# Expert blocks with the weights as the loaded operand of gate and up

## Chip, cores and metric

The kernel runs on one core of one Trainium2 chip. The time is device time of one execution in microseconds; the three runs before the change took 1558.29, 1562.61 and 1563.08 us, so the median is 1562.61.

## What is computed

Four sub-layers follow each other on 2048 tokens of 512 numbers, each added to its input and normalised: a linear attention, a feed-forward layer with int8 weights, a cumulative gate, and a mixture of 32 experts. The change touches the last one:

```python
router_probs = jax.nn.softmax(x @ gate_weight.T)
# 8 experts a token, some rerouted by a similarity matrix; combine = weight of each expert for each token
def expert_step(y, params):
    wgu, wd, cw = params          # (384, 512), (512, 192), (2048,)
    gu = x @ wgu.T
    g, u = jnp.split(gu, 2, axis=-1)
    h = jax.nn.silu(g) * u
    y = y + h @ wd.T * cw[:, None]
```

## The kernel before, in words

The program is written engine by engine; each engine runs its instructions in the order of the code, and semaphores join them. The first three sub-layers and the routing take the first 930 us or so. Routing sorts the 2048 x 8 pairs of token and expert into 159 blocks (NBLK) of 128 rows with one expert each. `every_block` (line 348 is its loop) then runs the same code for each block on every engine: eight blocks written out, a loop of eight blocks a turn, and the rest written out.

Numbers are held as two halves of 16 bits, high and low, so a product is three matmuls: high x high, high x low, low x high. `products` lists them with the four pieces of 128 of the 512 inputs: 12 for gate and up.

For a block k, POOL gathers its 128 rows (L1794). TensorE turns them (`gather_transposes`, L880, eight turns: four pieces, high and low), VectorE copies them out (L1341). `gate_up` (L889) is on TensorE the product with the tokens as loaded operand and the 384 columns of gate and up streaming past; tokens come out on partitions. ScalarE makes silu of the gate columns (L1619), VectorE multiplies by up and by the token's weight for this expert (L1351), ScalarE copies the high half (helper line L1380), VectorE subtracts for the low half (L1353, L1354). `h_transposes` (L899) turns h, three turns, ScalarE copies that out (L1380, the 384-wide form), and `expert_down` (L910) makes five matmuls of 512 columns. ScalarE copies y out with a constant scale (L1380, 512 wide), POOL adds its rows into memory (L1801).

On TensorE the code of one block k is in this order: down of block k-3; the waits for the expert's weights (L923, L924) and the turned rows; two thirds of gate/up; the turns of block k+1's rows; the last third; the turns of h of block k-1. The wait in `h_transposes` is for `h_lo`, VectorE's last subtraction.

The weights of the experts lie in eight slots. Which slot a block uses is known only when the kernel runs: the expert's number comes out of packed words, which TensorE and VectorE read into registers (L357, `load_words`; TensorE at the first and third block of eight), and the place of a piece is the slot's number times its size plus a constant:

```python
def weights(sl, j, c0, n):
    return Wslot[:, bass.ds(sl * (2 * WCOLS) + (j * WCOLS + c0), n)]
```

Such a place is computed by an instruction of the engine's sequencer, called ISA in the order of instructions and FUSED_REGOPS in the trace, ahead of the first matmul that reads it.

Of the kernel before, what the change touches and what calls it, by code (L numbers as in the profile page):

```python
# [24 lines left out]
P = 128  # L25
# [59 lines left out]
def build(nc, ins, out):  # L85
    ctx = ExitStack()
    with ctx:
# [88 lines left out]
        def wc(a, k, c0, n):  # L176
# [61 lines left out]
        xTb = [r.take([2 * KD, P], F16) for _ in range(2)]  # L238
        sgD = [r.take([DFF], F32) for _ in range(2)]
        h32 = [r.take([DFF], F32) for _ in range(2)]  # L240
        hB = [r.take([3 * P], F16) for _ in range(2)]
        hT = [r.take([3, P], F16) for _ in range(2)]
# [44 lines left out]
        w_in, xg_in, y_out = sem("w_in"), [sem(f"xg_in{i}") for i in range(NG)], [sem(f"y_out{i}") for i in range(2)]  # L287
        xt_ready, xt_sb, gu_ready, sg_ready, h_ready, h_hi, h_lo, ht_ready, ht_sb, blk_done, y_sb = (sem(n) for n in (
            "xt_ready", "xt_sb", "gu_ready", "sg_ready", "h_ready", "h_hi", "h_lo", "ht_ready", "ht_sb", "blk_done", "y_sb"))
        fin_in, fin_first, sum_ready = [sem(f"fin_in{i}") for i in range(4)], sem("fin_first"), sem("sum_ready")  # L290
# [301 lines left out]
        def _(pe):  # L592
# [292 lines left out]

            def gate_up(k, sl, some):
                d = bank[2 + k.u % 2][:, 0:2 * DFF]
                for a, b, kd in some:
                    mm = pe.matmul(d, xTb[k.u % 2][:, a * KD + kd, :], weights(sl, b, kd * 2 * DFF, 2 * DFF),  # L889
                                   start=(a, b, kd) == (0, 0, 0), stop=(a, b, kd) == (1, 0, KD - 1))  # L890
                return mm

            def h_transposes(k):
                pe.wait_ge(h_lo, k.i + 1)
                if not k.before(2):
                    pe.wait_ge(ht_sb, k.i - 1)
                d = bank[4 + k.u % 2][:, :].bitcast(F16)
                for c in range(3):
                    mm = pe.transpose(d[:, c * P:(c + 1) * P], hB[k.u % 2][:, c * P:(c + 1) * P], ident16[:, :])  # L899
                mm.then_inc(ht_ready, 1)  # L900

            def expert_down(k, sl):
                pe.wait_ge(ht_sb, k.i + 1)
                if not k.before(2):
                    pe.wait_ge(y_sb, k.i - 1)
                d = bank[6 + k.u % 2][:, :]
                base = KD * 2 * DFF
                order = ((1, 0, base), (1, 1, base), (0, 0, base), (2, 0, base + DIM), (2, 1, base + DIM))
                for n, (c, j, c0) in enumerate(order):
                    mm = pe.matmul(d, hT[k.u % 2][:, c, :], weights(sl, j, c0, DIM), start=n == 0, stop=n == 4)  # L910
                mm.then_inc(blk_done, 1)
# [4 lines left out]
            def expert_block(k, fresh, last=False):  # L916
                if fresh:
                    held["packs"] = load_words(pe.engine, k, 0, 1)
                e = expert_of(held["packs"], k.u)
                if not k.before(3):  # L920
                    expert_down(k.at(-3), expert_of(held["packs"], k.u - 3) % NSLOT)
                sl = e % NSLOT
                pe.wait_ge(w_in, e * 32 + 32)  # L923
                pe.wait_ge(xt_sb, k.i + 1)  # L924
                if not k.before(2):
                    pe.wait_ge(h_ready, k.i - 1)
                gate_up(k, sl, products[:6])
                if k.u == 2:
                    held["packs"] = held["packs"] + load_words(pe.engine, k, 1, 2)
                gate_up(k, sl, products[6:8])  # L930
                if not last:
                    gather_transposes(k.at(1))
                gate_up(k, sl, products[8:]).then_inc(gu_ready, 1)
                if not k.before(1):
                    h_transposes(k.at(-1))

# [3 lines left out]
            every_block(pe, 8, expert_block, 8)  # L940
            final = [Blk(0, NBLK - j, 8) for j in (3, 2, 1)]
            expert_down(final[0], expert_of(held["packs"], NBLK % 8 - 3) % NSLOT)
            h_transposes(final[2])
            expert_down(final[1], expert_of(held["packs"], NBLK % 8 - 2) % NSLOT)
            expert_down(final[2], expert_of(held["packs"], NBLK % 8 - 1) % NSLOT)


        @block.vector
        def _(dve):
# [334 lines left out]
            choices(3)  # L1284
            own.did(dve.memset(xgs[:, :, DIM:XROW], 0.0))
            one_hots(2, 0, 12)
            candidates(3)
# [55 lines left out]
            def expert_block(k, fresh, last=False):  # L1343
                if not last:
                    xt_evac(k.at(1))
                if fresh:
                    mine["packs"] = load_words(dve.engine, k, 0, 2)
                cw = xg[k.u % NG].bitcast(F32)[:, DIM:XROW][:, bass.ds(expert_of(mine["packs"], k.u), 1)]
                h, split = h32[k.u % 2], hB[k.u % 2]
                dve.wait_ge(sg_ready, k.i + 1)  # L1350
                dve.scalar_tensor_tensor(h, bank[2 + k.u % 2][:, DFF:2 * DFF], cw, sgD[k.u % 2], ALU.mult, ALU.mult).then_inc(h_ready, 1)  # L1351
                dve.wait_ge(h_hi, k.i + 1)
                dve.tensor_tensor(split[:, 0:P], h[:, 0:P], split[:, P:2 * P], ALU.subtract)  # L1353
                dve.tensor_tensor(split[:, 2 * P + 64:3 * P], h[:, P:DFF], split[:, 2 * P:2 * P + 64], ALU.subtract).then_inc(h_lo, 1)  # L1354

# [17 lines left out]
        def _(act):  # L1373
# [228 lines left out]

            def ht_evac(k):
                act.wait_ge(ht_ready, k.i + 1)
                if not k.before(2):
                    act.wait_ge(blk_done, k.i)
                copy(hT[k.u % 2].rearrange("p c n -> p (c n)"), bank[4 + k.u % 2][:, :].bitcast(F16)[:, 0:3 * P]).then_inc(ht_sb, 1)
# [22 lines left out]
            ht_evac(Blk(0, NBLK - 1, 8))  # L1630
            y_evac(Blk(0, NBLK - 2, 8))
# [276 lines left out]
```

## Time and profile before

| | |
|---|---|
| median of three runs | 1562.61 us |
| profiled execution | 1556.97 us, its span 1555.1 us |
| TensorE busy | 1405.1 us, 90% of the span |
| VectorE, ScalarE, GpSimd busy | 909.7, 662.7, 763.6 us |
| mean granted TensorE clock | 0.954 |

PE is TensorE's matmuls, PEld its weight loads, which run beside them; PEldq and PEq are its sequencer, which issues both, computes addresses and waits for semaphores, and whose rows count in no busy time. DVE is VectorE, ACT ScalarE, POOL GpSimd. A matmul's row lasts from its issue to its modelled end, so rows overlap: its own cost in a run of them is the step from start to start. The clock is a share of the upper level.

### The profile page before, as it was taken

The numbers are of one execution on the slowest core, as the hardware profiler recorded it, in microseconds if no ns is written. First come the engines' busy times: TensorE is split into PE (matmuls) and PEld (weight loads), VectorE is DVE, ScalarE is ACT, GpSimd is POOL, SyncE is SP. The second block draws the span as 40 slices with busy tenths as digits, with TensorE's granted clock in tenths as the row PEclk, the third lists the DMA queues.
The fourth block names the chain that finished last, engine by engine and source line by source line (L and its number), as shares of the span: only waits on it lengthen the run. The fifth ranks groups of instructions, "written<-read, shape, count | busy, mean of one in ns | idle before, by whom it ended". The sixth has DMA issues, their size and how long they took to land.

```text
span 1555.1 us, 31694 instructions
## 1 busy us (share of the span) xinstructions
PE 1405.1 (90%) x10327; PEld 771.1 (50%) x10328; DVE 909.7 (58%) x1826; ACT 662.7 (43%) x1250; POOL 763.6 (49%) x691
## 2 busy tenths in 40 slices
PE   5799899799999999999886359999999999999990
PEld 2455555444444444445443226666666666666650
DVE  7677566676757676635988864444444444444435
ACT  6332222455454545423444424444444444444443
POOL 3565454510100101233645446777777677777655
PEclk9999999899999999999998569999999999999995
DMA  8777666689696969432303636888888988776767
GB/s 273 170 156 187 120 111 122 150 297 311 223 295 224 299 229 297 169 107 82 83 18 100 200 120 121 174 172 199 192 192 175 207 188 191 142 113 90 177 80 230
DMA packets 213452, 271.72 MB, mean 175 GB/s; under 512 B 133993, under 2 KB 135561, under 8 KB 212368
## 3 DMA queue, kind: packets, MB, share of 16 engines
q1 hardware_dynamic: 177776, 211.40, 46.6%
q0 software_dynamic: 35616, 59.58, 23.5%
q8 instruction: 31, 0.51, 0.1%
q14 instruction: 29, 0.24, 0.0%
HBM read 158.92 MB, written 101.71 MB: 168 GB/s over the span
## 4 chain that ended last, share of the span: by engine, by line
PE 73%; DVE 13%; DMA 5%; issue 2%; ACT 2%; POOL 2%; SPq 2%; DVEq 0%; ACTq 0%; POOLq 0%
PE bank L889 20%; PE bank L910 11%; PE bank L716 7%; PE bank L722 6%; PE bank L739 6%; PE bank L598 6%; PE bank L880 5%; PE bank L606 4%; DMA ARENA<-ARENA 4%; PE bank L673 2%; PE bank L899 2%; DVE ARENA L1251 1%; PE bank L818 1%; DVE bs L956 1%; DVE WA L1197 1%
## 5 line engine op out<-in xcount | busy, mean ns | idle before, releaser
L889 PE MATMUL bank<-ARENA,XT 128*128 x1908 | 364.0, 327 | 2.5 <-issue 1.4
L1801 POOL DMA_INDIRECT accs<-X,WA x159 | 252.3, 1587 | 89.6 <-issue 42.0
L889 PEld LDWEIGHTS bank<-ARENA,XT 128*128 128x128 f16 x1908 | 180.4, 98 | 124.5 <-issue 8.5
L1341 DVE COPY XT<-bank 128x1024 f16<-128x1024 f16 x159 | 110.0, 692 | 179.0 <-PE bank L880 146.2
L1794 POOL DMA_INDIRECT XT<-x_rows,WA x159 | 166.6, 1048 | 97.1 <-issue 42.1
L910 PE MATMUL bank<-ARENA,XT 128*128 x795 | 197.4, 379 | 0.8 <-issue 0.7
L1380 ACT ACTIVATE ARENA<-ARENA 128x512 f16<-128x512 f32 (+2 forms) x128 | 89.2, 708 | 231.7 <-DVE ARENA L1099 130.6
L1619 ACT ACTIVATE XT<-bank 128x192 f32<-128x192 f32 x159 | 52.5, 330 | 286.7 <-PE bank L889 232.7
L598 PE MATMUL bank<-XT,STG 128*128 128x512 f16 x640 | 152.4, 386 | 7.7 <-DVE ARENA L1145 7.6
L1647 POOL TENSOR_TENSOR rstd<-mv,mhalf 128x1 f32<-128x1 f32 x28 | 5.7, 202 | 281.9 <-DVE mv L959 281.9
L606 PE MATMUL bank<-WA,XT 128*128 128x512 f16 x540 | 126.2, 384 | 0.0
L716 PE MATMUL bank<-XT,WA 128*128 (+1 forms) x512 | 122.3, 382 | 3.4 <-issue 3.4
L739 PE MATMUL bank<-ARENA 128*128 128x512 f16 x512 | 121.1, 379 | 3.5 <-DVE ARENA L1105 3.4
L1351 DVE SCALAR_TENSOR_TENSOR XT<-bank,XT 128x192 f32<-128x192 f32 x159 | 66.4, 418 | 98.2 <-ACT XT L1619 65.4
L722 PE MATMUL bank<-XT,ARENA 128*128 (+1 forms) x512 | 120.9, 379 | 0.0
L598 PEld LDWEIGHTS bank<-XT,STG 128*128 128x128 f16 x640 | 62.8, 99 | 81.2 <-DVE ARENA L1145 9.0
L880 PE MATMUL bank<-ident,XT 128*128 128x128 f16 x1272 | 97.8, 220 | 5.6 <-DMA XT<-x_rows,WA 5.6
L1656 POOL TENSOR_TENSOR ARENA<-X,ARENA 128x512 f16<-128x512 f32 (+1 forms) x48 | 63.6, 1338 | 78.4 <-ACT ARENA L1380 78.4
L910 PEld LDWEIGHTS bank<-ARENA,XT 128*128 128x128 f16 x795 | 71.6, 98 | 57.7 <-issue 1.8
L880 PEld LDWEIGHTS bank<-ident,XT 128*128 128x128 f16 x1272 | 85.0, 98 | 25.7 <-issue 6.2
L1380 ACT ACTIVATE X<-bank 128x512 f32<-128x512 f32 x159 | 93.3, 587 | 2.8 <-PE bank L910 1.3
L953 DVE SCALAR_TENSOR_TENSOR WA<-ARENA,WA 128x1280 f16<-128x1280 f32 x48 | 73.3, 1527 | 25.5 <-ACT WA L1380 25.5
(244 smaller groups left out, 2184.6 us busy)
## 6 DMA issues: line engine op xcount, KB each, us to landing
w_scratch<-WA SPq DMA_DIRECT2D x64, 640.0 KB, 3.9
ARENA<-w_scratch SPq DMA_DIRECT2D x64, 640.0 KB
ARENA<-w_exp SPq DMA_DIRECT2D x48, 640.0 KB, 5.3
WA<-w_exp SPq DMA_DIRECT2D x16, 640.0 KB, 5.0
ARENA<-ARENA SPq DMA_DIRECT2D x32, 256.0 KB, 3.5
accs<-ARENA SPq DMA_DIRECT2D x20, 256.0 KB, 3.4
X<-x SPq DMA_DIRECT2D x4, 1024.0 KB, 6.8
ARENA<-wc SPq DMA_DIRECT2D x8, 512.0 KB, 6.0
```

Source lines behind the costliest of these rows:

```text
L598: mm = pe.matmul(dst, wa(a, k), wb(b, k), start=n == 0, stop=n == 3 * KD - 1)
L606: mm = pe.matmul(bank[j][:, :], XT[:, a, k, tk], Wqkv[:, b, k, j * DIM:(j + 1) * DIM], start=n == 0, stop=n == 3 * KD - 1)
L716: mm = pe.matmul(bank[0][:, :], Wg[:, n % KD, m * P:(m + 1) * P], XT[:, n // KD, n % KD, tk], start=n == 0, stop=n == 2 * KD - 1)
L722: mm = pe.matmul(bank[1 + m % 2][:, :], Wu[:, n % KD, m * P:(m + 1) * P], XT[:, n // KD, n % KD, tk], start=n == 0, stop=n == 2 * KD - 1)
L739: mm = pe.matmul(bank[4 + tt][:, :], fB[:, m % 2, a, tt * P:(tt + 1) * P], Wd[:, m, :], start=m == 0 and a == 0, stop=m == NM - 1 and a == 1)
L880: mm = pe.transpose(d[:, c * P:(c + 1) * P], xg[k.u % NG].bitcast(F16)[:, c * P:(c + 1) * P], ident16[:, :])
L889: mm = pe.matmul(d, xTb[k.u % 2][:, a * KD + kd, :], weights(sl, b, kd * 2 * DFF, 2 * DFF), start=(a, b, kd) == (0, 0, 0), stop=(a, b, kd) ...
L910: mm = pe.matmul(d, hT[k.u % 2][:, c, :], weights(sl, j, c0, DIM), start=n == 0, stop=n == 4)
L1341: dve.tensor_copy(xTb[k.u % 2].rearrange("p c n -> p (c n)"), bank[k.u % 2][:, :].bitcast(F16)).then_inc(xt_sb, 1)
L1380: return act.activation(dst, src, ACT.Copy, scale=scale)
L1794: pool.indirect_dma_start(xg[i % NG], None, xrows, bass.IndirectOffsetOnAxis(blkidx[:, i:i + 1], 0), bounds_check=TOK - 1, oob_is_err=Fals ...
L1801: pool.indirect_dma_start(accs, bass.IndirectOffsetOnAxis(blkout[:, i:i + 1], 0), yD[i % 8], None, compute_op=ALU.add).then_inc(y_out[i % ...
```

## The change

Gate and up are computed with the weights as the loaded operand and the tokens streaming, so features come out on partitions, in three parts of 128 (gate 0 to 127; gate 128 to 191 with up 0 to 63; up 64 to 191). h then lies as the down product needs it: its turns and their copy go. The multiply by up is three instructions, two of them between different halves of the partitions. The token's weight, which can't be multiplied along partitions now, goes into the scale of the copy of y. The down product runs two blocks behind in place of three.

```diff
-        sgD = [r.take([DFF], F32) for _ in range(2)]
-        h32 = [r.take([DFF], F32) for _ in range(2)]
-        hB = [r.take([3 * P], F16) for _ in range(2)]
+        sgD = [r.take([2 * P], F32) for _ in range(2)]
+        h32 = [r.take([2 * P], F32) for _ in range(2)]
+        cwS = small[:, 108:116]
...
-            def gate_up(k, sl, some):
-                d = bank[2 + k.u % 2][:, 0:2 * DFF]
+            def gate_up(k, sl, part, some):
+                d = bank[2 + k.u % 2][:, part * P:(part + 1) * P]
                 for a, b, kd in some:
-                    mm = pe.matmul(d, xTb[k.u % 2][:, a * KD + kd, :], weights(sl, b, kd * 2 * DFF, 2 * DFF),
+                    w = weights(sl, b, kd * 2 * DFF + part * P, P)
+                    mm = pe.matmul(d, w, xTb[k.u % 2][:, a * KD + kd, :],
                                    start=(a, b, kd) == (0, 0, 0), stop=(a, b, kd) == (1, 0, KD - 1))
...
-            def h_transposes(k):
...
             def expert_down(k, sl):
-                pe.wait_ge(ht_sb, k.i + 1)
+                pe.wait_ge(h_lo, k.i + 1)
...
-                if not k.before(3):
-                    expert_down(k.at(-3), expert_of(held["packs"], k.u - 3) % NSLOT)
+                if not k.before(2):
+                    expert_down(k.at(-2), expert_of(held["packs"], k.u - 2) % NSLOT)
...
-                gate_up(k, sl, products[:6])
+                gate_up(k, sl, 0, products)
                 if k.u == 2:
                     held["packs"] = held["packs"] + load_words(pe.engine, k, 1, 2)
-                gate_up(k, sl, products[6:8])
+                gate_up(k, sl, 1, products)
                 if not last:
                     gather_transposes(k.at(1))
-                gate_up(k, sl, products[8:]).then_inc(gu_ready, 1)
-                if not k.before(1):
-                    h_transposes(k.at(-1))
+                gate_up(k, sl, 2, products).then_inc(gu_ready, 1)
...
+            for h in h32:
+                own.did(dve.memset(h[:, P:2 * P], 0.0))
...
+                dve.tensor_scalar(cwS[:, k.u % 8:k.u % 8 + 1], cw, 1 / (WS * WS), None, ALU.mult)
                 dve.wait_ge(sg_ready, k.i + 1)
-                dve.scalar_tensor_tensor(h, bank[2 + k.u % 2][:, DFF:2 * DFF], cw, sgD[k.u % 2], ALU.mult, ALU.mult).then_inc(h_ready, 1)
+                dve.tensor_tensor(h[0:64, 0:P], d[64:128, P:2 * P], sg[0:64, 0:P], ALU.mult)
+                dve.tensor_tensor(h[64:128, 0:P], d[0:64, 2 * P:3 * P], sg[64:128, 0:P], ALU.mult)
+                dve.tensor_tensor(h[0:64, P:2 * P], d[64:128, 2 * P:3 * P], sg[0:64, P:2 * P], ALU.mult).then_inc(h_ready, 1)
                 dve.wait_ge(h_hi, k.i + 1)
-                dve.tensor_tensor(split[:, 0:P], h[:, 0:P], split[:, P:2 * P], ALU.subtract)
-                dve.tensor_tensor(split[:, 2 * P + 64:3 * P], h[:, P:DFF], split[:, 2 * P:2 * P + 64], ALU.subtract).then_inc(h_lo, 1)
+                dve.tensor_tensor(turned[:, 0, :], h[:, 0:P], turned[:, 1, :], ALU.subtract)
+                dve.tensor_tensor(turned[64:128, 2, :], h[0:64, P:2 * P], turned[0:64, 2, :], ALU.subtract).then_inc(h_lo, 1)
...
-                copy(yD[k.u % 8], bank[6 + k.u % 2][:, :], 1 / (WS * WS)).then_inc(y_sb, 1)
+                act.activation(yD[k.u % 8], bank[6 + k.u % 2][:, :], ACT.Copy, scale=cwS[:, k.u % 8:k.u % 8 + 1]).then_inc(y_sb, 1)
...
-                act.activation(sgD[k.u % 2], bank[2 + k.u % 2][:, 0:DFF], ACT.Silu, scale=1 / WS).then_inc(sg_ready, 1)
-                if not k.before(1):
-                    ht_evac(k.at(-1))
+                act.activation(sgD[k.u % 2], bank[2 + k.u % 2][:, 0:2 * P], ACT.Silu, scale=1 / WS).then_inc(sg_ready, 1)
                 act.wait_ge(h_ready, k.i + 1)
                 if not k.before(2):
-                    act.wait_ge(ht_ready, k.i - 1)
-                copy(hB[k.u % 2][:, P:2 * P + 64], h32[k.u % 2]).then_inc(h_hi, 1)
+                    act.wait_ge(blk_done, k.i)
+                copy(hT[k.u % 2][:, 1:3, :].rearrange("p c n -> p (c n)"), h32[k.u % 2]).then_inc(h_hi, 1)
```

TensorE's instructions from the eighth gate/up matmul of a block of the loop to the next block's down product, before; `ident` is the unit matrix for a turn, `bank` the result, XT the tokens, ARENA the weight slots, and in brackets stands what is waited for:

```order
L889 ISA
L889 MATMUL bank<-ARENA,XT 128x384
L875 ISA
L880 MATMUL bank<-ident,XT 128x128 [waits xt_sb,xg_in1]
L880 MATMUL bank<-ident,XT 128x128 x7
L889 MATMUL bank<-ARENA,XT 128x384 x4
L899 MATMUL bank<-ident,XT 128x128 [waits ht_sb,h_lo]
L899 MATMUL bank<-ident,XT 128x128 x2
L905 REGISTER_ALU [waits ht_sb]
L910 ISA [waits y_sb]
L910 REGISTER_ALU
```

The same stretch of the same block with the change, from the end of the second part of gate/up (it begins and ends between addresses that go on in the same way):

```order
L890 ISA
L890 MATMUL bank<-XT,ARENA 128x128 x5
L875 ISA
L880 MATMUL bank<-ident,XT 128x128 [waits xt_sb,xg_in1]
L880 MATMUL bank<-ident,XT 128x128 x7
L890 ISA
L890 MATMUL bank<-XT,ARENA 128x128
L890 ISA
L890 MATMUL bank<-XT,ARENA 128x128
```

Behind the turns, where four matmuls without an ISA stood, the third part begins with its own eight, one ahead of each of its first eight matmuls; the last of these is the `x5` row, the eighth and the four that use places again. The turns of h are gone, and `h_lo` is waited for at the down product:

```order
L890 ISA
L890 MATMUL bank<-XT,ARENA 128x128 x5
L897 REGISTER_ALU [waits h_lo]
L902 ISA [waits y_sb]
L902 REGISTER_ALU
L902 MATMUL bank<-ARENA,XT 128x512
```

In the eight blocks of the loop's body there are 64 rows `L889 ISA` before and 192 rows `L890 ISA` with the change; the 32 of the down product stay.

On VectorE one block of the loop is before:

```order
L1341 COPY XT<-bank 128x1024 [waits gu_ready,xt_ready]
L1351 ISA [waits sg_ready]
L1351 SCALAR_TENSOR_TENSOR XT<-bank,XT 128x192
L1353 TENSOR_TENSOR XT<-XT 128x128 [waits h_hi]
L1354 TENSOR_TENSOR XT<-XT 128x64
```

and with the change:

```order
L1330 COPY XT<-bank 128x1024 [waits gu_ready,xt_ready]
L1339 ISA
L1339 TENSOR_SCALAR small<-XT 128x1
L1341 TENSOR_TENSOR XT<-bank,XT 64x128 [waits sg_ready]
L1342 TENSOR_TENSOR XT<-bank,XT 64x128
L1343 TENSOR_TENSOR XT<-bank,XT 64x128
L1345 TENSOR_TENSOR XT<-XT 128x128 [waits h_hi]
L1346 TENSOR_TENSOR XT<-XT 64x128
```

The address of the token's weight is now computed before the wait for `sg_ready`, and three multiplies stand behind that wait in place of one.

## Rows read from the trace of the kernel before

**Rows 1.** The page: busy time by engine; the chain that ended last, by engine.

```profile
PE 1405.1 (90%) x10327; PEld 771.1 (50%) x10328; DVE 909.7 (58%) x1826; ACT 662.7 (43%) x1250; POOL 763.6 (49%) x691
...
PE bank L889 20%; PE bank L910 11%; PE bank L716 7%; PE bank L722 6%; PE bank L739 6%; PE bank L598 6%; PE bank L880 5%; PE bank L606 4%; DMA ARENA<-ARENA 4%; PE bank L673 2%; PE bank L899 2%; DVE ARENA L1251 1%; PE bank L818 1%; DVE bs L956 1%; DVE WA L1197 1%
```

**Rows 2.** Stretches: us, busy PE, PEld, DVE, ACT, POOL, clock, DMA share, GB/s.

```profile
0.00:100.00 100.00, 73.09 (x762) 38.23 (x767) 73.45 (x100) 48.14 (x64) 49.08 (x38) 0.93 0.79 205
...
985.00:1483.00 498.00, 496.73 (x3808) 310.18 (x3806) 209.16 (x544) 218.29 (x544) 358.12 (x272) 1.00 0.82 168
```

**Rows 3.** The chain in order of time, one block: start, us, what.

```profile
1204.11 1.30 PE bank L889 x8
1205.41 0.45 PE bank L880 x8
1205.86 0.65 PE bank L889 x4
1206.51 0.17 PE bank L899 x3
1206.67 1.08 PE bank L910 x5
```

**Rows 4.** Lines L889 (whole span), L923 (984 to 1483): durations min/median/max, first, last start.

```profile
L889 PE MATMUL bank<-ARENA,XT x1908: 326/326/524, 928.1 to 1509.6; 128*128 x191
L889 PEldq FUSED_REGOPS  x1272: 46/46/96, 928.0 to 1507.9; - x182
...
L923 PEldq FUSED_REGOPS  x136: 83/135/142, 987.0 to 1479.8; - x136
```

**Rows 5.** The same view: runs of addresses ahead of the array, L889 and L606.

```profile
L889 PEldq FUSED_REGOPS  x8: 46/46/91, 1213.9 to 1214.9; - x8
...
L889 PEldq FUSED_REGOPS  x6: 46/46/57, 1217.9 to 1218.5; - x6
...
L606 PEldq FUSED_REGOPS  x8: 46/46/51, 72.5 to 73.4; - x8
```

**Rows 6.** The same view: sequencer rows around 951, 1220 and 1230 us.

```profile
L877 PEldq EVENT_SEMAPHORE  x1: 51/51/51, 951.0 to 951.0; - x1
...
L896 PEldq EVENT_SEMAPHORE  x1: 51/51/51, 951.2 to 951.2; - x1
...
L348 PEldq ALU_OP  x1: 32/32/32, 1219.4 to 1219.4; - x1
...
L903 PEldq FUSED_REGOPS  x1: 47/47/47, 1220.5 to 1220.5; - x1
...
L923 PEldq FUSED_REGOPS  x2: 83/90/98, 1228.4 to 1231.5; - x2
...
L357 PEldq FUSED_REGOPS  x2: 46/98/151, 1229.5 to 1230.0; - x2
...
L357 PEldq SEQ_ASSERT  x1: 18/18/18, 1230.2 to 1230.2; - x1
```

**Rows 7.** The same view: L637 and L638 at 78 to 80 us; groups by line: one load.

```profile
L637 PE MATMUL bank<-ARENA x16: 219/219/219, 78.4 to 80.1; 128*128 128x128 f16 x16
...
L638 PE MATMUL bank<-ARENA x16: 219/219/219, 78.5 to 80.1; 128*128 128x128 f16 x16
...
L880 PEld LDWEIGHTS bank<-ident,XT 128*128 128x128 f16 x1054 | 69.9, 98 | 16.4
```

**Rows 8.** Groups of VectorE and ScalarE, 1000 to 1480 us: busy, mean ns, idle before.

```profile
L1341 DVE COPY XT<-bank 128x1024 f16<-128x1024 f16 x131 | 90.6, 692 | 140.7 <-PE bank L880 115.2 <-issue 25.4
L1351 DVE SCALAR_TENSOR_TENSOR XT<-bank,XT 128x192 f32<-128x192 f32 x131 | 54.8, 418 | 80.6 <-ACT XT L1619 52.5 <-issue 28.1
L1353 DVE TENSOR_TENSOR XT<-XT 128x128 f16<-128x128 f32 x131 | 38.3, 293 | 56.9 <-ACT XT L1380 50.5 <-issue 6.4
...
L1380 ACT ACTIVATE X<-bank 128x512 f32<-128x512 f32 x131 | 76.9, 587 | 1.1 <-PE bank L910 0.4
L1380 ACT ACTIVATE XT<-bank 128x384 f16<-128x384 f16 x131 | 63.7, 486 | 5.5 <-PE bank L899 4.9
```

More of the change, by code:

```diff
@@ L287, in build @@
         w_in, xg_in, y_out = sem("w_in"), [sem(f"xg_in{i}") for i in range(NG)], [sem(f"y_out{i}") for i in range(2)]
-        xt_ready, xt_sb, gu_ready, sg_ready, h_ready, h_hi, h_lo, ht_ready, ht_sb, blk_done, y_sb = (sem(n) for n in (
-            "xt_ready", "xt_sb", "gu_ready", "sg_ready", "h_ready", "h_hi", "h_lo", "ht_ready", "ht_sb", "blk_done", "y_sb"))
+        xt_ready, xt_sb, gu_ready, sg_ready, h_ready, h_hi, h_lo, blk_done, y_sb = (sem(n) for n in (
+            "xt_ready", "xt_sb", "gu_ready", "sg_ready", "h_ready", "h_hi", "h_lo", "blk_done", "y_sb"))
         fin_in, fin_first, sum_ready = [sem(f"fin_in{i}") for i in range(4)], sem("fin_first"), sem("sum_ready")
@@ L884, in weights, with expert_down @@
                 return Wslot[:, bass.ds(sl * (2 * WCOLS) + (j * WCOLS + c0), n)]
-            def gate_up(k, sl, some):
-                d = bank[2 + k.u % 2][:, 0:2 * DFF]
+            def gate_up(k, sl, part, some):
+                d = bank[2 + k.u % 2][:, part * P:(part + 1) * P]
                 for a, b, kd in some:
-                    mm = pe.matmul(d, xTb[k.u % 2][:, a * KD + kd, :], weights(sl, b, kd * 2 * DFF, 2 * DFF),
+                    w = weights(sl, b, kd * 2 * DFF + part * P, P)
+                    mm = pe.matmul(d, w, xTb[k.u % 2][:, a * KD + kd, :],
                                    start=(a, b, kd) == (0, 0, 0), stop=(a, b, kd) == (1, 0, KD - 1))
                 return mm
-            def h_transposes(k):
+            def expert_down(k, sl):
                 pe.wait_ge(h_lo, k.i + 1)
[L895 to L902, printed above, removed]
-                pe.wait_ge(ht_sb, k.i + 1)
                 if not k.before(2):
@@ L940, in _ @@
             every_block(pe, 8, expert_block, 8)
[L941 to L945, printed above, removed]
+            for j in (2, 1):
+                expert_down(Blk(0, NBLK - j, 8), expert_of(held["packs"], NBLK % 8 - j) % NSLOT)
         @block.vector
@@ L1348, in expert_block @@
                 cw = xg[k.u % NG].bitcast(F32)[:, DIM:XROW][:, bass.ds(expert_of(mine["packs"], k.u), 1)]
-                h, split = h32[k.u % 2], hB[k.u % 2]
+                d, sg, h, turned = bank[2 + k.u % 2], sgD[k.u % 2], h32[k.u % 2], hT[k.u % 2]
+                dve.tensor_scalar(cwS[:, k.u % 8:k.u % 8 + 1], cw, 1 / (WS * WS), None, ALU.mult)
                 dve.wait_ge(sg_ready, k.i + 1)
-                dve.scalar_tensor_tensor(h, bank[2 + k.u % 2][:, DFF:2 * DFF], cw, sgD[k.u % 2], ALU.mult, ALU.mult).then_inc(h_ready, 1)
+                dve.tensor_tensor(h[0:64, 0:P], d[64:128, P:2 * P], sg[0:64, 0:P], ALU.mult)
+                dve.tensor_tensor(h[64:128, 0:P], d[0:64, 2 * P:3 * P], sg[64:128, 0:P], ALU.mult)
+                dve.tensor_tensor(h[0:64, P:2 * P], d[64:128, 2 * P:3 * P], sg[0:64, P:2 * P], ALU.mult).then_inc(h_ready, 1)
                 dve.wait_ge(h_hi, k.i + 1)
-                dve.tensor_tensor(split[:, 0:P], h[:, 0:P], split[:, P:2 * P], ALU.subtract)
-                dve.tensor_tensor(split[:, 2 * P + 64:3 * P], h[:, P:DFF], split[:, 2 * P:2 * P + 64], ALU.subtract).then_inc(h_lo, 1)
+                dve.tensor_tensor(turned[:, 0, :], h[:, 0:P], turned[:, 1, :], ALU.subtract)
+                dve.tensor_tensor(turned[64:128, 2, :], h[0:64, P:2 * P], turned[0:64, 2, :], ALU.subtract).then_inc(h_lo, 1)
             xt_evac(Blk(0, 0, 8))
@@ L1601, in _ @@
             copy(region, bank[2][:, 256:256 + NBLK]).then_inc(region_sb, 1)
[L1603 to L1607, printed above, removed]
             def y_evac(k):
@@ L1629, in _ @@
             every_block(act, 8, expert_block)
-            ht_evac(Blk(0, NBLK - 1, 8))
             y_evac(Blk(0, NBLK - 2, 8))
```

## The prediction

> **What bounds the kernel now.** I read the page first: TensorE is busy 90% of the span, and the chain that ended last goes through it most, with the expert blocks' gate/up line L889 at its head [rows 1]. The change touches only these blocks, so next I read the table of stretches: from 985 to 1483 us TensorE has work 496.7 of 498.0 us at granted clock 1.00, its upper level of 2.4 GHz [rows 2]. Then the chain in order of time shows one block with no gap in it: 8 gate/up matmuls of 384 columns in 1.30 us, 8 turns of gathered rows in 0.45, 4 more gate/up in 0.65, 3 turns of h in 0.17, 5 down matmuls in 1.08, together 3.65 us [rows 3]. That is also the pace of the address row L923, issued once a block: 135 steps from 987.0 to 1479.8, 3.65 us each [rows 4]. So the array's columns set the block today: 162 ns a gate/up matmul, 56 ns a turn, 216 ns a down matmul [rows 3].
>
> What a busy array hides is who feeds it. TensorE's sequencer issues in order, and a block's weights lie in a slot that a register names, so an address is computed (FUSED_REGOPS in the trace, ISA in the order of instructions) before a matmul that reads a new place of the slot: 1272 for L889, 8 a block [rows 4]. Each lasts 46 ns, but they don't follow each other every 46 ns. Where the sequencer runs free, ahead of the array, eight in a row start from 1213.9 to 1214.9 and six from 1217.9 to 1218.5; in the attention stage, where the loaded operand is the one with the register, eight go from 72.5 to 73.4 [rows 5]. That is 0.14, 0.12 and 0.13 us a step; I take 0.125, since the 0.14 includes a longer first row. The same pace holds with one matmul behind each address or several (in the 72.5 run, five follow the fourth), so the address has the price, not the matmul: from L877 to L896 twelve load-and-matmul pairs without a new address are issued in 0.2 us [rows 6], of which 0.05 is the wait's own row: 0.012 us a pair.
>
> Today this is hidden. In a block where the sequencer was catching up, L923 follows L923 after 3.1 us, of which 0.75 goes to a word load (1229.5 to just past 1230.2) [rows 6]: 2.35 us of issue against 3.65 of columns.
>
> **The change part by part.**
>
> *Gate/up turned round.* 12 matmuls of 384 columns become 36 of 128. Columns: 36 x 0.056 = 2.02 us against 12 x 0.1625 = 1.95, +0.07 [rows 3]. That each carries its own weight load costs nothing on the array: in the attention stage 32 such pairs, L637 and L638 in turn, start from 78.4 to 80.1, some 55 ns each, with loads of 98 ns beside them [rows 7]. Against that stands a rule of the Trainium skill, TensorE: Matmul & The Clock Gate, section Back-to-back issue gap: a sustained stream of load-and-matmul pairs at 128 columns runs at about 81 ns a pair, which as an estimate would make this block 44 x 0.081 + 1.08 = 4.64 us on the array and the kernel about 1715 us. The 32 pairs disagree, and I go by them.
>
> Issue: 24 new addresses a block in place of 8 (each third of the 384 features has eight places, and the low-part product reuses the last four). 16 x 0.125 = +2.0 us. Eight more pairs without an address add 8 x 0.012 = 0.1.
>
> *h_transposes and their copy go.* TensorE loses 3 x 0.056 = 0.17 us of columns, its sequencer about 0.1 us (three pairs and a wait, by the L877 row). ScalarE loses a copy of 0.49 us [rows 8]; the array never stood still for it, so that is worth nothing.
>
> *Sum for a block.* Array: 2.02 + 0.45 + 1.08 = 3.55 us. Issue: 2.35 + 2.0 + 0.1 - 0.1 = 4.35. The sequencer becomes the bound. It then also shows what it hid so far, once in eight blocks: the loop's branch and first word load, 1219.4 to 1220.5 or 1.1 us, and the second load, 0.75 [rows 6]; 1.85 / 8 = 0.23. Together 4.58 us; the branch's first row partly overlaps what the block before had queued, so I take 4.56.
>
> *VectorE.* One multiply of 0.42 us becomes three of half the partitions, by the rows between 0.29 and 0.42 each, and a one-column scaling; one subtraction grows from 64 to 128 columns. Sums 0.7 to 1.1 us more a block, on an engine with 209 of 498 us busy [rows 2, 8]: hidden while its chain stays short. *ScalarE*: a sigmoid-times-x pass 64 columns wider, a copy 64 wider, the token weight as scale of the copy that it did anyway: under 0.2 us, and 0.49 gone. Two fills before the blocks are under 0.5 us. POOL's and SP's instructions stay.
>
> *The down product moves* from three blocks behind to two, and its wait for h_lo now stands on the sequencer before everything of the block. Behind it queue the five down matmuls, then gate/up. After the last gate/up of block k-2 comes the whole issue of block k-1, 4.56 us, before that wait. The chain meanwhile is activation 0.49 at most, three multiplies 1.26, copy 0.49, two subtractions 0.58: 2.8 us, and 4.1 if both engines first finish another copy (0.59 and 0.69) [rows 8]. It fits; cost nothing, and up to 0.5 us in the one block of eight with VectorE's own word load if it doesn't (10 us in all).
>
> **Total.** 159 blocks x (4.56 - 3.65) = +145 us on the profiled execution's 1557.0: 1702 us. The median of the three runs is 5.6 above that execution and all lie within 1558 to 1563, so I say **1704 us**. An address at 0.12 or 0.13 moves this by 24 x 0.005 x 159 = 19 us either way, the rounding of the other rows by 16: 1670 to 1738.
>
> **The rivals.**
>
> *The array keeps the pace (the other side).* If an address cost the sequencer little more than its 46 ns, the array would bound: 3.55 us, 159 x 0.10 = 16 us less, 1541. It decides at (3.55 - 2.56) / 16 = 62 ns an address, 2.56 being all that is issued without the 16. For it: the 46 ns of the rows, and that the trace may itself slow this sequencer. Against it: three runs of addresses in two stages, none under 0.12 [rows 5]. Between 62 and 69 ns it would be no change.
>
> *TensorE's clock falls.* The array would have 3.55 of 4.56 us to do, 78%. From 0 to 100 us, with 73% busy, the granted clock was 0.93 [rows 2], so some 0.14 of the time at the lower level of 1.2 GHz. There a block's columns take 7.1 us, more than its issue: 5% on 725 us, 38 us more, 1740. Against it: no idle stretch is longer than an address's step.
>
> *Weight loads don't overlap.* At 98 ns a pair [rows 7] the array takes 44 x 0.098 + 1.08 = 5.39 us a block, +277 us, 1834. The 32 pairs at 56 speak against it. The rule named above lies between the two.
>
> *The chain is late after all*: 1704 plus up to 10, as above.
>
> **How the numbers follow.** Forecast 0.78; clock 0.07; loads 0.03; chain 0.03; array bound 0.06, and 0.03 for an address price in between, near no change. A measurement tells about 0.3% from no change here. Faster 0.06, same 0.02, slower 0.92 (the in-between case split between the last two). The range, 1660 to 1745, holds the forecast with its roundings, the chain and the clock case; it leaves out the array bound, the loads and some of the edges, under 0.2.
>
> **What would show it.** L890 addresses at 24 a block, 3816 in all, 0.12 to 0.13 us apart throughout, not only in short runs; the gate/up matmuls with addresses starting 0.125 us apart and the four without 0.056; one block 4.3 to 4.4 us, a pair of blocks of eight a full us longer; TensorE idle with "issue" as its reason; the turns of h gone from every list; VectorE some 0.7 to 1.1 us busier a block and waited for by nobody. Wrong would be: gate/up pairs 56 ns apart with the block at 3.55 us; addresses closer than 0.1 us; h_lo or xt_sb named as what TensorE waited for; a granted clock under 0.95 through the blocks.

## The result: slower, 1723.4 us

The changed kernel takes 1723.36 us (median of four runs, 1722.40 to 1724.31) against 1562.84 us before in the same measurement: a ratio of 1.1033, with a 95% interval of 1.1019 to 1.1048. The forecast was 1704, between 1660 and 1745. The page of the profile after, busy time by engine and the head of the chain by line:

```profile
PE 1530.2 (89%) x13666; PEld 953.0 (55%) x13667; DVE 1022.9 (59%) x2305; ACT 626.8 (36%) x1091; POOL 763.8 (44%) x691
...
PE bank L890 26%; PE bank L902 10%; PE bank L716 5%; PE bank L722 5%; PE bank L739 5%; PE bank L598 5%; PE bank L880 4%; PE bank L606 4%; DMA ARENA<-ARENA 2%; PE bank L673 2%; DVE ARENA L1238 1%; ACT ARENA L1372 1%; DVE bs L943 1%; PE bank L818 1%; DVE WA L1184 1%
```

By the share of busy time nothing has happened: TensorE 89% where it was 90% [rows 1]. A matmul's row lasts 219 ns however soon the next one follows, so rows that start 125 ns apart still touch. The table of stretches has the same trap (columns as in [rows 2]):

```profile
985.00:1483.00 498.00, 474.19 (x5238) 364.99 (x5235) 239.28 (x748) 146.49 (x321) 282.20 (x214) 1.00 0.70 143
```

474 of 498 us have a matmul under way, but only 107 blocks go through the stretch in place of 136. The granted clock is 1.00 in both. What changed is seen in the rows of the gate/up line and of the address row that is issued once a block (durations min/median/max, first and last start; then what TensorE's idle time waited for):

```profile
L890 PE MATMUL bank<-XT,ARENA x5724: 219/219/314, 933.3 to 1676.3; 128*128 128x128 f16 x198
L890 PEldq FUSED_REGOPS  x3816: 46/46/96, 933.1 to 1676.0; - x191
its engine sat idle before it (us, times) until:
  issue: 44.3, 140
  DVE XT L1330: 4.3, 4
...
L915 PEldq FUSED_REGOPS  x159: 82/135/162, 932.1 to 1672.5; - x159
```

There are 3816 addresses, 24 a block, each 46 ns long as before [rows 4]. The blocks' own row goes 158 steps in 740.4 us, so a block takes **4.69 us** over all and 4.66 in the loop, in place of 3.65 [rows 4]. Idle time of TensorE is "issue", hardly ever another engine. The chain in order of time shows where a block's time lies:

```profile
1256.60 1.08 PE bank L902 x5
1257.68 2.07 PE bank L890 x24
1259.74 0.45 PE bank L880 x8
1260.19 0.71 PE bank L890 x12
1260.90 1.08 PE bank L902 x5
1261.98 2.04 PE bank L890 x24
1264.02 0.45 PE bank L880 x8
1264.46 0.71 PE bank L890 x12
1265.17 0.03 issue
1265.20 1.25 PE bank L902 x5
1266.45 2.07 PE bank L890 x24
1268.52 0.45 PE bank L880 x8
1268.96 0.80 PE bank L890 x12
1269.76 1.28 issue
1271.04 1.24 PE bank L902 x5
```

The first two thirds of gate/up, 24 matmuls with 16 addresses, take 2.04 to 2.07 us where their columns need 24 x 0.056 = 1.34: this is the pace of addresses. The turns, which need one address at most, stay at 0.45 and let the sequencer get a little ahead; the last third uses that up and takes 0.71. From one down product to the next it is 4.30 us in the first two blocks, and 5.84 in the one that holds the loop's branch and first word load.

### The profile page after: what moved, and what is told of

It is laid out like the page before. It is cut to its first block, busy times and chain, and to the rows that moved or that the text cites. A ratio compares the mean times of both kernels' runs of the same rounds, so it can differ in the third digit from the quotient of the medians.

```text
span 1722.0 us, 40922 instructions
## 1 busy us (share of the span) xinstructions
PE 1530.2 (89%) x13666; PEld 953.0 (55%) x13667; DVE 1022.9 (59%) x2305; ACT 626.8 (36%) x1091; POOL 763.8 (44%) x691
## 4 chain that ended last, share of the span: by engine, by line
PE 72%; DVE 13%; issue 5%; DMA 4%; ACT 3%; POOL 2%; SPq 1%; another core or an unknown queue 0%; DVEq 0%; ACTq 0%; POOLq 0%
PE bank L890 26%; PE bank L902 10%; PE bank L716 5%; PE bank L722 5%; PE bank L739 5%; PE bank L598 5%; PE bank L880 4%; PE bank L606 4%; DMA ARENA<-ARENA 2%; PE bank L673 2%; DVE ARENA L1238 1%; ACT ARENA L1372 1%; DVE bs L943 1%; PE bank L818 1%; DVE WA L1184 1%
## 5 line engine op out<-in xcount | busy, mean ns | idle before, releaser
L890 PE MATMUL bank<-XT,ARENA 128*128 128x128 f16 x5724 | 504.6, 223 | 13.0 <-issue 8.4
L890 PEld LDWEIGHTS bank<-XT,ARENA 128*128 x5724 | 406.9, 97 | 116.6 <-issue 35.9
L902 PE MATMUL bank<-ARENA,XT 128*128 x795 | 197.8, 379 | 27.3 <-issue 24.4
L1605 ACT ACTIVATE XT<-bank 128x256 f32<-128x256 f32 x159 | 61.1, 384 | 364.7 <-PE bank L890 243.2
L1330 DVE COPY XT<-bank 128x1024 f16<-128x1024 f16 x159 | 110.0, 692 | 134.7 <-PE bank L880 119.5
L1341 DVE TENSOR_TENSOR XT<-bank,XT 64x128 f32<-64x128 f32 x159 | 46.6, 293 | 161.9 <-ACT XT L1605 154.7
L1372 ACT ACTIVATE XT<-XT 128x256 f16<-128x256 f32 x159 | 66.2, 417 | 177.1 <-DVE XT L1343 174.1
L606 PE MATMUL bank<-WA,XT 128*128 128x512 f16 x540 | 125.3, 382 | 0.0
L902 PEld LDWEIGHTS bank<-ARENA,XT 128*128 128x128 f16 x795 | 76.8, 97 | 86.1 <-issue 36.0
L1599 ACT ACTIVATE X<-bank,small 128x512 f32<-128x512 f32 x159 | 106.5, 671 | 1.0 <-PE bank L902 1.0
L1345 DVE TENSOR_TENSOR XT<-XT 128x128 f16<-128x128 f32 x159 | 46.6, 293 | 76.7 <-ACT XT L1372 67.0
```

What stands on the lines that cost most here:

```text
L606: mm = pe.matmul(bank[j][:, :], XT[:, a, k, tk], Wqkv[:, b, k, j * DIM:(j + 1) * DIM], start=n == 0, stop=n == 3 * KD - 1)
L890: mm = pe.matmul(d, w, xTb[k.u % 2][:, a * KD + kd, :], start=(a, b, kd) == (0, 0, 0), stop=(a, b, kd) == (1, 0, KD - 1))
L1330: dve.tensor_copy(xTb[k.u % 2].rearrange("p c n -> p (c n)"), bank[k.u % 2][:, :].bitcast(F16)).then_inc(xt_sb, 1)
L1372: return act.activation(dst, src, ACT.Copy, scale=scale)
```

## The experiments

The times of all fourteen kernels, with the ratio where there is more than one run. A block is a turn of the loop divided by eight, from the trace (of e3 and e4, whole blocks from first to last address row).

| kernel | us | ratio to before (95%) | block, us |
|---|---|---|---|
| before | 1562.8 | | 3.65 |
| after | 1723.4 | 1.1033 (1.1019 to 1.1048) | 4.66 |
| e1 after, addresses packed | 1629.6 | 1.0443 (1.0421 to 1.0465) | 4.10 |
| e2 after, no gate/up addresses | 1608.8 | one run | 3.95 |
| e3 before, gate/up in thirds | 1777.6 | one run | 5.01 |
| e4 before, addresses packed | 1559.6 | 0.9986 (0.9975 to 0.9998) | 3.66 |
| e5 e1, down three behind | 1583.1 | 1.0130 (1.0108 to 1.0151) | 3.77 |
| e6 after, down three behind | 1737.2 | 1.1116 (1.1091 to 1.1141) | 4.75 |
| e7 e1, waits for its own gate/up | 1782.1 | 1.1384 (1.1355 to 1.1413) | 5.09 |
| e8 e1, three operations an address | 1722.3 | one run | 4.69 |
| e9 e1, no scatter | 1560.2 | 0.9992 (0.9980 to 1.0005) | 3.70 |
| e10 e5, reordered | 1568.9 | 1.0042 (1.0024 to 1.0061) | 3.70 |
| e11 e8, down three behind | 1692.2 | one run | 4.47 |
| e12 e10, down at the block's end | 1570.3 | 1.0064 (1.0046 to 1.0083) | 3.75 |

### e1 and e2: the addresses taken away

An address here is three operations on registers (add, times two bytes, add the base). On a view in bytes it needs one, and when all are computed together, up to six operations share an instruction: e1's trace has 5 address instructions a block for gate/up in place of 24.

```diff
 def weights(sl, j, c0, n):
-    return Wslot[:, bass.ds(sl * (2 * WCOLS) + (j * WCOLS + c0), n)]
+    return Wslot.bitcast(I8)[:, bass.ds(sl * (4 * WCOLS) + 2 * (j * WCOLS + c0), 2 * n)].bitcast(F16)
...
 pe.wait_ge(w_in, e * 32 + 32)
+for part in range(3):
+    for b in range(2):
+        for kd in range(KD):
+            pe.lower_ap(weights(sl, b, kd * 2 * DFF + part * P, P), for_matmul_weights=True)
```

> The changed kernel, with a block's 24 gate/up addresses computed together at the head of the block and the slot taken on a view in bytes, so that an address is one operation on registers in place of three: 5 address instructions a block in place of 24, the same matmuls, loads and waits. Theory A (the sequencer's addresses bound the changed block): 19 fewer addresses at 0.125 us take 2.4 us of issue from a block of 4.66 us, which leaves some 2.3, less than the array's 3.55; the array bounds again, 1723 - 159 x (4.66 - 3.55) = 1547 us, between 1540 and 1565, and gate/up matmuls start 55 to 57 ns apart. Rival B (an operand named by a register, or a new weight load for each 128 columns, is what takes the array 0.125 us): nothing changes, 1715 to 1730. Rival C (the down product, now two blocks behind, waits for h_lo as soon as the block is shorter): h_lo stands behind a chain of 2.4 to 2.8 us against 3.55 less what lies between; the block stops between 3.6 and 4.2 us, 1555 to 1650, and h_lo is named as TensorE's wait.

e2 takes every load from the unit matrix:

```diff
-w = weights(sl, b, kd * 2 * DFF + part * P, P)
+w = ident16[:, :]
```

> The changed kernel, with every gate/up load taken from one fixed place (the unit matrix) in place of the expert's slot: no gate/up address at all, the same number of loads, matmuls and waits. It leaves out reading the experts' gate and up weights, so gate and up are not the experts'. Theory A (addresses bound): issue about 1.6 us a block, the array bounds at 3.55 us, about 1547 us (1540 to 1565); with e1 the same within 10 us. Rival B1 (44 load-and-matmul pairs in a row cost about 0.08 us each on the array, whatever the address): block 4.6 us, about 1715. Rival B2 (it is the register in the load itself that is slow, not the instruction that computes it): e2 falls to 1547 while e1 stays near 1723.

Measured: 1629.6 and 1608.8 us. Neither stayed near 1723, so rival B falls in all its forms: the same matmuls with the same loads from the same registers go faster when fewer instructions compute addresses. The array's own pace shows in e2's chain:

```profile
1210.63 1.08 PE bank L902 x5
1211.71 1.34 PE bank L890 x24
1213.05 0.45 PE bank L880 x8
1213.50 0.67 PE bank L890 x12
```

24 load-and-matmul pairs in 1.34 us are 56 ns each, 32 with the turns behind them in 1.79. The Trainium skill, TensorE: Matmul & The Clock Gate, section Back-to-back issue gap, has about 81 ns for such a stream; this trace differs, and the measurement decides.

But neither came to 1547. In e1 the down product's idle time (view of line L902) is

```profile
L902 PEldq ALU_OP  x598: 32/32/36, 938.6 to 1581.7; - x200
L902 PEldq FUSED_REGOPS  x38: 182/188/200, 963.7 to 1557.2; - x38
its engine sat idle before it (us, times) until:
  issue: 64.0, 79
  DVE XT L1350: 42.5, 64
```

L1350 is `h_lo`, the last subtraction. Rival C is there as soon as the block gets short: the gaps ahead of the down product come to 0.40 us a block (985 to 1483 us), the loop's branch included, and to 0.08 in e9, where that wait is gone. It is a cost that the addresses had covered.

### e3 and e4: the same in the kernel before

e3 leaves the tokens as loaded operand and only cuts gate/up into thirds, so that 24 addresses are computed:

```diff
-mm = pe.matmul(d, xTb[k.u % 2][:, a * KD + kd, :], weights(sl, b, kd * 2 * DFF, 2 * DFF),
+mm = pe.matmul(d, xTb[k.u % 2][:, a * KD + kd, :], weights(sl, b, kd * 2 * DFF + part * P, P),
```

> The kernel before, with tokens still as loaded operand, the turns of h kept and the down product three blocks behind, but gate/up in three parts of 128 columns, one after the other: 36 matmuls and 24 addresses a block in place of 12 and 8, nothing else changed. Theory A (addresses bound): the block is as slow as the changed kernel's plus the issue of the turns of h, 4.66 to 4.8 us, so 1563 + 159 x (1.01 to 1.15) = 1724 to 1746. Rival (the weights as loaded operand, or the new chain behind them, made the changed kernel slow): columns 36 x 0.056 against 12 x 0.1625 are 0.07 us a block more, so 1574 us, 1563 to 1585.

e4 packs the 8 addresses of the kernel before, with e1's view in bytes and

```diff
+for b in range(2):
+    for kd in range(KD):
+        pe.lower_ap(weights(sl, b, kd * 2 * DFF, 2 * DFF))
```

> The kernel before, with its 8 gate/up addresses a block computed together and on the byte view: 2 address instructions a block in place of 8, some 0.7 us a block less to issue, nothing else changed. If the array's columns bound it, as the prediction read it, no change: 1563 within 5 us. If issue bounds it in part (at the block in eight with the loop's branch and its first word load), up to 0.7 us in one or two of eight blocks: 14 to 28 us faster.

e3 took 1777.6 us: the loss is there without the turned product, without the new chain and with the turns of h kept, so it belongs to the 24 addresses. It went past its range, with 5.01 us a block and not 4.66 to 4.8. Two things in its sequencer's rows were not in my sum: the turns of h bring waits with them, and from a wait to the next row the sequencer needs 0.125 us, as for an address; and the step behind the last wait ahead of gate/up takes 0.34 us in the mean, where after has 0.12. e4 took 1559.6, within its 5 us: with 162 ns a matmul the addresses of before were hidden.

### e5 and e6: the down product three blocks behind again

Four buffers of h in place of two, and

```diff
-if not k.before(2):
-    expert_down(k.at(-2), expert_of(held["packs"], k.u - 2) % NSLOT)
+if not k.before(3):
+    expert_down(k.at(-3), expert_of(held["packs"], k.u - 3) % NSLOT)
```

in the packed kernel (e5) and in the changed one (e6).

> The packed kernel (e1, 1630 us, block 4.10), with the down product three blocks behind gate/up again in place of two, and four buffers of h in place of two, so that the wait for h_lo has a whole block more. In e1 some 0.5 us a block are a wait for h_lo at the head of the down product. If that wait is all that is left over the array's 3.55 us: 1547 us, 1540 to 1565. If VectorE's order (the copy of the turned rows stands behind the subtractions of the block before) then becomes what the array waits for: 3.7 to 3.9 us, 1570 to 1605, with xt_sb named. If the late product wasn't the cause: 1630.

> The changed kernel with its 24 addresses a block, the down product three blocks behind again and four buffers of h; nothing packed. Theory A (addresses bound the changed block, the wait for h_lo adds at most 0.08 us a block): 1710 to 1723. Rival (the change's loss lies in the late chain, and e1 gained only because packing moved the issue): 1560 to 1640.

With e1 and after these make a square: packing is worth 94 us two blocks behind (1723 to 1630) and 154 three behind (1737 to 1583); the third block is worth 47 us with packed addresses and costs 14 without. So the addresses bound the changed kernel, and the wait for h only decides once they are gone. e6's rival, that the late chain was the loss, is out. That e6 is slower by 14 us I had not expected. Between 985 and 1483 us the step at the wait for `h_lo` did shrink, from 0.19 to 0.13 us in the mean (10 us over 159 blocks), but the step behind the waits ahead of gate/up grew from 0.12 to 0.24 (19 us). That leaves some 5 us open. The idle time of L890 names the copied rows (L1330, `xt_sb`) 17 times, where after has 4:

```profile
  issue: 63.0, 149
  DVE XT L1330: 10.0, 17
```

e5 kept 0.22 us a block over the array's 3.55: 0.11 behind the down product (three in a turn of the loop), 0.09 ahead of it (one in each turn).

### e8 and e11: is the price by operation or by instruction?

e8 is e1 without the byte view, so 13 address instructions a block, of up to six operations; e11 is e8 with e5's edit, the down product three behind.

```diff
-return Wslot.bitcast(I8)[:, bass.ds(sl * (4 * WCOLS) + 2 * (j * WCOLS + c0), 2 * n)].bitcast(F16)
+return Wslot[:, bass.ds(sl * (2 * WCOLS) + (j * WCOLS + c0), n)]
```

> The packed kernel e1 without the view in bytes: the gate/up addresses are computed together at the head of the block, but each takes three operations on registers again, two addresses an instruction: 13 address instructions a block, all of six operations or three, in place of 24 (1723 us) or 5 (e1, 1630 us). If the price is by instruction, 0.13 us: 11 fewer than the changed kernel's, 1.4 us less issue, 3.2 us, under what bounds e1: 1630, within 15. If the price is by operation (72 and more in any case): near 1723. In between, at 0.16 us for one of six operations: 3.6 us, still under e1's 4.10.

> e8 (addresses computed together, three operations each, 13 instructions a block, 1722 us) with the down product three blocks behind. e8's 13 address instructions follow each other in 0.133 us, so the price is by instruction; but they stood as 1.7 us in one piece behind the wait for h_lo, with 1.08 us of down columns to cover them. If that place was the cause: with h_lo no longer waited for, the sequencer issues ahead and the block comes to 3.75 to 4.0 us, 1580 to 1620. If the operations cost and not the instructions: 1700 to 1725.

Both missed: 1722.3 and 1692.2 us. The price itself is in the sequencer's rows. In e8

```profile
L919 PEldq FUSED_REGOPS  x2052: 42/74/115, 930.6 to 1672.0; - x187
```

they last 74 ns in place of 46, and follow each other every 133 ns in the median (139 in e1), against 124 ns for three operations in after and 113 ns for the single ALU_OP of e1's down product. Six operations cost little more than one: the price is by instruction. The miss is in the place. Thirteen in one piece are 1.7 us, and the array had less than that in store. In e11, around 1208 us:

```profile
L902 PE MATMUL bank<-ARENA,XT x5: 379/379/379, 1207.9 to 1208.8; 128*128 x5
...
L919 PEldq FUSED_REGOPS  x13: 42/74/110, 1207.8 to 1209.5; - x13
...
L890 PE MATMUL bank<-XT,ARENA x3: 217/218/218, 1209.7 to 1209.8; 128*128 128x128 f16 x3
```

The last down matmul is over at 1209.0, the addresses at 1209.6, and the array waits 0.66 us; over the loop it is 0.78 us a block. How far the sequencer gets ahead can be counted: matmuls that stand ahead of its row in the program and start after it. At e11's wait ahead of the down product it is 17 in every block of the loop but the first of each turn, behind the branch, where it is 0. Between 985 and 1483 us it is 17 at the same place in 95 of 132 blocks of e5, and at L896 in 100 of 136 of the kernel before, never more. Seventeen matmuls of 384 columns are 2.8 us; of 128 columns, 0.95 us. In after it is 4 in 70 of 107 blocks, which are the four without an address at the end of gate/up, and 0 to 2 in the others: no lead at all. That is how an issue-bound stretch looks. (The Trainium skill, Advanced Engine Details and Errata, section Engine Queue Depths, gives TensorE a queue depth of 64; 17 matmuls with their loads are 34 instructions, so the measurement is what I go by.)

### e7 and e9: why h is late

In e1 the wait for h falls on every second block, and its cause is not the length of the chain. Around 1206 us in e1:

```profile
L890 PE MATMUL bank<-XT,ARENA x12: 219/219/219, 1205.7 to 1206.3; 128*128 128x128 f16 x12
...
L902 PE MATMUL bank<-ARENA,XT x5: 379/379/379, 1206.3 to 1207.2; 128*128 x5
...
L1609 ACT ACTIVATE XT<-bank x1: 385/385/385, 1208.0 to 1208.0; 128x256 f32<-128x256 f32 x1
...
L1788 POOL DMA_INDIRECT accs<-X,WA x1: 1589/1589/1589, 1206.5 to 1206.5; - x1
```

Gate/up is through at 1206.5, ScalarE is free, and silu (L1609) starts at 1208.0: the trace's record of semaphores has gate/up's increment, by which TensorE tells ScalarE that the product is there, at 1207.95, 1.67 us after the last matmul's start, where the prompt value is 0.23. The down product's increment, of a matmul 0.92 us later, comes 0.07 us behind it, so the array itself was not late. My first idea was that an increment waits as long as further matmuls follow; e7 lets none follow:

```diff
 if not k.before(2):
+    pe.wait_ge(gu_ready, k.i)
     expert_down(k.at(-2), expert_of(held["packs"], k.u - 2) % NSLOT)
```

> The packed kernel e1, with one wait more on TensorE's sequencer: ahead of the down product it waits for its own last gate/up matmul. In e1 the increment that tells ScalarE of that matmul comes 0.23 us after its start where the array then pauses, but 1.6 to 1.8 us after it where the next matmuls follow at once, and silu starts that much later. Theory L (an increment is told late as long as matmuls without a pause follow it; the lateness, not the chain's own 2.4 to 2.8 us, makes h_lo late): every increment comes after 0.23 us, the pause costs 0.2 to 0.35 us a block, h_lo is in time: block 3.75 to 3.9, 1580 to 1605 us, faster than e1 by an added wait. Rival (the chain is too long by itself): the pause comes on top or changes nothing, 1630 to 1660.

1782.1 us, outside the rival's range too: theory L is wrong. The increment comes late with the array at rest as well, 1.17 us after the start in the median, and now TensorE waits for it and has an empty queue behind it. Idle time ahead of the down product (L902) in e7:

```profile
its engine sat idle before it (us, times) until:
  issue: 184.8, 160
  PE bank L890: 157.3, 150
```

The other thing that runs in those spans is GpSimd's scatter of y (1.59 us) or gather (1.05 us). Between 1000 and 1450 us, of TensorE's increments that fall due (their row ends) 0.4 to 1.4 us after a scatter's start, 53 of 63 in e1 and 77 of 79 in e7 come more than 0.15 us late, mostly about 1.5 us after the scatter's start; of ScalarE's 0 of 23 and of VectorE's 0 of 59 in e1. e9 leaves the scatter out:

```diff
-pool.indirect_dma_start(accs, bass.IndirectOffsetOnAxis(blkout[:, i:i + 1], 0), yD[i % 8], None,
-                        compute_op=ALU.add).then_inc(y_out[i % 2], 16)
+pool.memset(blkout[:, i:i + 1], 0).then_inc(y_out[i % 2], 16)
```

> The packed kernel e1 (1630 us, down product two blocks behind), with GpSimd's scatter of y left out: in its place GpSimd writes zero to one column that nothing reads any more and gives the same increment. It leaves out adding the experts' results into memory, so the output has no expert part. In e1 and e7 TensorE's increments that fall due while GpSimd works on the scatter (1.59 us a block) come some 1.5 us after that scatter's start, be the array pausing or not; ScalarE's and VectorE's come at once. Theory G (the scatter holds TensorE's increments, and that makes h_lo late in e1): the gate/up increments come 0.23 us after the matmul's start, the wait for h_lo shrinks, block 3.6 to 3.8 us: 1550 to 1582. Rival (coincidence: both follow y's copy, and the increments are late for another reason): 1615 to 1640, increments still 1.5 to 1.8 us late in every second block.

1560.2 us, inside theory G's range and 69 under e1. The wait for `h_lo` is gone, once in place of 64 times (L902 again):

```profile
  issue: 22.8, 39
  DVE XT L1350: 1.5, 1
```

Gate/up's increments still come at 0.50 us in the median, not at 0.23; the gather is still there. That TensorE's late increments, and with them the wait for `h_lo`, go when the scatter goes is shown; whether GpSimd's work on it holds them or the transfers that it starts is not, since both went. Nor does the scatter do it alone. By the same count 38 of 134 are late in the kernel before and 28 of 125 in e4, where gate/up streams 384 columns, but 66 of 66 in after and 183 of 184 in e3, which keeps the tokens as loaded operand and only cuts gate/up into matmuls of 128 columns. What it is in the short matmuls that makes the difference, no run here separates.

### e10 and e12: can the turned product win?

On e5, e10 puts the next block's turns to the head of the block, and VectorE's copy of them behind the multiplies of the block before:

```diff
+if not last:
+    gather_transposes(k.at(1))
 sl = e % NSLOT
...
-if not last:
-    xt_evac(k.at(1))
...
+if not k.past(2):
+    xt_evac(k.at(2))
 dve.wait_ge(h_hi, k.i + 1)
```

> e5 (packed, three behind, 1583 us, block 3.77 us; over the array's 3.55 it has 0.11 us of waits behind the down product, mostly for the copy of the turned rows, and 0.09 ahead of it, one in each turn of the loop at its branch and word load). The turns of the next block's rows go to the head of the block, ahead of gate/up, and VectorE's copy of them from ahead of the multiplies of the block before to behind them, into the time in which ScalarE copies h. If the turned rows come in time then: 3.63 to 3.68 us, 1560 to 1569 us, level with the kernel before. If the increments held by GpSimd still make them late: 1575 to 1590. Under 1558, faster than before, only if the wait at the loop's branch goes too.

e12 moves the down product of block k-2 to the end of block k, and the turns ahead of both word loads:

```diff
-if not k.before(3):
-    expert_down(k.at(-3), expert_of(held["packs"], k.u - 3) % NSLOT)
...
 gate_up(k, sl, 2, products).then_inc(gu_ready, 1)
+if not k.before(2):
+    expert_down(k.at(-2), expert_of(held["packs"], k.u - 2) % NSLOT)
```

> e10 (1569 us, block 3.70 us; what is left over the array's 3.55 is one wait of 0.9 us in each turn of the loop, at its branch and word load, with nothing but 17 short matmuls issued ahead, 0.95 us of columns). The down product of block k-2 goes to the end of block k in place of the head of k+1, so that the 17 matmuls issued ahead at the branch hold its five of 512 columns (1.08 + 12 x 0.056 = 1.75 us), and the turns of the next block stand ahead of both word loads, since they need no word. If the sequencer's lead is counted in matmuls: the wait at the branch falls from 0.9 to 0.3 us or less, block 3.58 to 3.64 us, 1552 to 1561 us, the same as the kernel before or up to 0.7% faster. If the lead is a fixed time: no change, 1565 to 1572. If the increments held by GpSimd make h_lo late again: 1575 or more.

e10 took 1568.9 us, at the end of its first range. The waits for turned rows are gone; what is left is 0.115 us a block ahead of the down product, nearly all in the block behind the loop's branch (0.93 us there). e12 was to hide that and did not: 1570.3. The measured time lies where the expectation put a lead of a fixed time, but the lead at the wait ahead of the down product is 17 matmuls here as well (89 of 133 blocks between 985 and 1483 us). From that wait to the branch the sequencer needs 0.65 us for the down product's addresses, so its lead is partly spent when it gets there. The wait moved behind the turns, 0.84 us in that block, and the second word load came to light with 0.35. No turned version with a full result beats the kernel before. The best, e10, is 0.4% slower, for an array that would save 16 us.

## Why the prediction held, step by step

**The bound changed hands, as said.** Array 3.55 us a block, issue above it. e2's chain shows the 3.55 (1.08 + 1.34 + 0.45 + 0.67), e1 to e3 that it is the addresses that bound the changed kernel.

**The price of an address** was 0.125 us; the trace of after has 124 ns in the median of the 2247 steps within a third of gate/up between 985 and 1483 us, 131 in the mean, since the first three steps of a block take 169, 135 and 135 in the median and single ones up to 279. 24 x 0.006 = 0.14 us a block too little.

**Plain blocks** were to take 4.35 us; the six plain ones of eight take 4.28 to 4.61, 4.41 in the mean (medians by place in the loop). The longer steps added 0.14 and the wait for `h_lo` 0.07 (0.19 against 0.12 us for that step of the sequencer); the other pieces were rounded up by about as much as two thirds of that. That these nearly cancel is luck.

**Branch and word loads** were to cost 1.85 us in eight blocks. The two blocks take 5.88 and 4.97, 2.0 us over two plain ones, though as 1.5 and 0.6 and not a full us each: 0.25 a block against 0.21 taken. Together 4.66 against 4.56, and 0.10 x 159 = 16 us of the 19 missing. The other 3 are the base of the sum: it sets out from the profiled execution's 1557.0 us and adds 2 of the 5.6 us by which the median of the runs lies above it; with all of them it is about 1707. The profiled execution of after also begins late, with its first gate/up matmul at 933.3 in place of 928.1 [rows 4], but the change adds only two fills before the blocks, and their first turn varies from 925.7 to 934.2 us over the profiled runs.

**The moved down product** was costed at nothing, at most 10 us: 0.07 x 159 = 11 us. The chain was sized right, 2.4 us in the median from silu's start to the end of the last subtraction against 2.8, but the increment that starts it can come up to 1.8 us late, which the rows that the forecast goes by do not show. From the last gate/up matmul it is 3.7 us in the median and up to 5.2. It stayed small because the block was long: e1 shows 0.40 us a block in the same place.

**The engines beside.** VectorE 0.7 to 1.1 us more a block: (1022.9 - 909.7) / 159 = 0.71, by multiplies of 284 to 294 ns, the low end. ScalarE was to lose 0.3; it lost 0.23, because of a term that I had at nothing, the scale of y's copy. With a scale read for each partition it takes

```profile
L1599 ACT ACTIVATE X<-bank,small 128x512 f32<-128x512 f32 x159 | 106.5, 671 | 1.0 <-PE bank L902 1.0
```

671 ns where the constant scale took 587 [rows 8]. TensorE does not wait for it.

**The rivals.** The array did not keep the pace: nothing in the 46 ns of an address's row says that the next can follow. The clock stayed at 1.00 in the blocks. Weight loads overlap, at 56 ns a pair. The chain was late by 11 us.

## What to carry to other kernels

Cost a register-addressed operand by the step from one address instruction to the next (0.11 to 0.14 us here), not by its row, and compare a block's count of them with its columns before a matmul is cut into smaller ones: 24 at 128 columns lose where 8 at 384 are free. Compute addresses together and with few operations, but in pieces that the queue can cover; its lead is a number of matmuls, so shorter matmuls give less time. A busy TensorE can hide a late signal and a chain that is a block too short; when the bound goes, look for what stands right behind it, here GpSimd's indirect DMA.

## Not expected of the hardware

- TensorE's semaphore increments come up to 1.8 us late while GpSimd works on an indirect scatter, in the kernel before too, though fewer (38 of 134 that fall due 0.4 to 1.4 us after a scatter's start, against 66 of 66 in after), and there nobody was in a hurry. None of ScalarE's and VectorE's was held in e1. The mechanism stays open.
- An address instruction of TensorE's sequencer costs 0.11 to 0.14 us whether it does one register operation, three or six, and a wait among addresses 0.12 to 0.13.
- At the waits where it was counted, the sequencer never had more than 17 matmuls issued ahead, whether short ones alone (e5, e11) or ones of 384 and 128 columns mixed (before).
